# Expert stage: gate and up projections four blocks ahead in one PSUM bank, token rows turned six ahead, sixteen weight places

## The reference

```python
x = x + attn(xn, w_qkv, w_proj) + ffn(xn, router_w, shared..., experts...)

logits = hidden @ router_w                         # 64 experts
affinity = sigmoid(logits)
top_scores, top_idx = top_k(affinity, 8)           # 8 experts a token
top_w = top_scores / (sum(top_scores) + 1e-9)
gate_out = einsum('bsh,ehi->bsei', hidden, expert_gate_k)   # 256 -> 128
up_out = einsum('bsh,ehi->bsei', hidden, expert_up_k)       # 256 -> 128
expert_act = silu(gate_out) * up_out
routed = einsum('bsei,eih->bsh', expert_act * router_mask[..., None], expert_down_k)
shared = (silu(hidden @ sgw) * (hidden @ suw)) @ sdw
```

## Time and profile before

| | before |
|---|---|
| median of 3 runs | 1426.3 us (1416.28 to 1426.62) |
| the profiled execution | 1423.97 us |
| its span, first to last instruction | 1421.5 us |
| TensorE busy | 1156.4 us, 81% |
| DVE busy | 795.5 us, 56% |
| ACT busy | 756.0 us, 53% |
| GpSimd busy | 648.6 us, 46% |
| mean granted TensorE clock | 0.96 |
| bytes moved by DMA | 213.85 MB, 150 GB/s on average |

### The profile page before, as it was taken

One profiled execution on the slowest core, in us unless ns is written; L12 is line 12 of the kernel. 1 busy time (PEld: TensorE's weight loads), 2 busy tenths in 40 slices (PEclk: granted clock), 3 DMA queues, 4 the chain that ended last, 5 costly groups with the idle time before them and its releaser, 6 DMA issues. The chain is left out here.

```text
span 1421.5 us, 35722 instructions
## 1 busy us (share of the span) xinstructions
PE 1156.4 (81%) x8297; PEld 818.3 (58%) x8298; DVE 795.5 (56%) x2512; ACT 756.0 (53%) x1914; POOL 648.6 (46%) x658
## 2 busy tenths in 40 slices
PE   6987994878788878788888789778787788887889
PEld 3543563777777777677777778333344444444447
DVE  7877893333333333333333334777777777777733
ACT  3554673555555555555555557255454454545553
POOL 1443144444444444444444443555555555555520
PEclk9999997899999999999999999799999999999999
DMA  7887002666666666666666653254544455544413
GB/s 223 219 213 195 12 12 74 184 195 189 176 197 191 194 197 174 187 189 193 194 204 204 195 165 121 87 132 121 134 120 117 110 138 120 134 115 113 116 44 119
DMA packets 143770, 213.85 MB, mean 150 GB/s; under 512 B 20193, under 2 KB 116449, under 8 KB 143714
## 3 DMA queue, kind: packets, MB, share of 16 engines
q1 hardware_dynamic: 115234, 126.38, 30.7%
q0 software_dynamic: 27648, 86.02, 23.3%
q10 hardware_dynamic: 832, 0.79, 0.2%
HBM read 243.26 MB, written 70.26 MB: 221 GB/s over the span
## 5 line engine op out<-in xcount | busy, mean ns | idle before, releaser
L1038 POOL DMA_INDIRECT xb<-token_rows,idx_ring_x x320 | 303.2, 947 | 334.4 <-DVE ys L1166 223.5
L1656 POOL DMA_INDIRECT yg<-expert_rows,idx_ring x256 | 265.5, 1037 | 207.9 <-PE psum L1365 119.3
L1069 PE MATMUL psum<-xTe,wgu 128*128 128x128 f32 x2560 | 348.2, 280 | 7.6 <-issue 7.6
L1486 ACT ACTIVATE pT<-psum 128x384 f32<-128x384 f32 (+1 forms) x512 | 211.2, 467 | 243.0 <-PE psum L1365 228.1
L1069 PEld LDWEIGHTS psum<-xTe,wgu 128*128 128x128 f32 x2560 | 319.8, 196 | 11.6 <-issue 11.6
L1079 PE MATMUL psum<-wb,aT 128*128 x640 | 204.4, 402 | 114.8 <-DVE aT L1157 97.7
L1551 DVE CUSTOM_DVE_ANT_0 masked<-psum,mask_q 128x384 f32<-128x384 f32 (+1 forms) x512 | 247.6, 519 | 89.6 <-PE psum L1372 81.7
L1157 DVE TENSOR_TENSOR aT<-gate,psum 128x128 f32<-128x128 f32 x320 | 91.6, 286 | 312.2 <-remote 112.7
L1166 DVE TENSOR_SCALAR ys<-psum,xb 128x256 f32<-128x256 f32 x320 | 154.7, 484 | 111.7 <-PE psum L1079 91.3
L1380 PE MATMUL psum<-qk 98*128 98x384 bf16 (+1 forms) x512 | 169.4, 332 | 55.7 <-ACT pT L1486 50.0
L1372 PE MATMUL psum<-qk 96*128 96x384 bf16 (+1 forms) x512 | 172.3, 339 | 41.3 <-DVE xT_all_or_onorm L1580 12.4
(11 more groups left out here) (143 smaller groups left out, 1121.8 us busy)
## 6 DMA issues: line engine op xcount, KB each, us to landing
wb<-in_w_exp SPq DMA_DIRECT2D x320, 384.0 KB
expert_rows<-ys SPq DMA_DIRECT2D x160, 256.0 KB
qk<-q_stacks SPq DMA_DIRECT2D x32, 384.0 KB
q_stacks<-wb SPq DMA_DIRECT2D x32, 192.0 KB, 2.7
qk<-k_parts SPq DMA_DIRECT2D x32, 192.0 KB
k_parts<-wb SPq DMA_DIRECT2D x28, 192.0 KB, 3.1
token_rows<-rows SPq DMA_DIRECT2D x8, 640.0 KB, 4.6
xb<-token_rows,idx_ring_x POOLq DMA_INDIRECT x320
```

Of the source, the lines that this page charges most:

```text
L1038: nc.gpsimd.indirect_dma_start(out=xb[:, r, :], out_offset=None, in_=rows_d, in_offset=bass.IndirectOffsetOnAxis(ap=idx_ring[:, q, r:r + 1 ...
L1069: last = nc.tensor.matmul(banks[bank + r % 2][:, 0:P], wgu[:, r % NW, h, part * I:(part + 1) * I], xT[:, r % 2, h, :], start=(h == 0), sto ...
L1486: nc.scalar.activation(pT[:, (j % 2) * HG + hh, 0:(hi - lo) * P], key_bank(j, hh)[:, 0:(hi - lo) * P], ACT.Exp).then_inc(p_ready, 1)
L1656: nc.gpsimd.indirect_dma_start(out=yg[:, h, k, :], out_offset=None, in_=y_d, in_offset=bass.IndirectOffsetOnAxis(ap=idx_ring[:, h, k:k + 1 ...
```

## The change

Gate and up of a block go to the two halves of one PSUM bank and raise one semaphore, `gu_ready`, after the last of them. The four banks G and U become four banks GU, taken by r % 4; `xT`, `gate` and `aT` have four buffers instead of two. In step r TensorE does down(r), turn_x(r + 6), gate_up(r + 4); ACT does silu(r + 3), copy_x(r + 6), copy_w(r + 6); DVE does take_y(r), product(r + 3). PX and Y keep two banks. `wb` gets 16 places instead of 8. The eight more, and `wgu`, lie in the memory of `xT_all_or_onorm`, which the stages before and after use; so the first 8 places are loaded in `route` as before, and SyncE loads the other 8 at the head of `experts`. From then on weights are loaded 16 blocks ahead.

```diff
-WR = 8
+WR = 16
+WARM = 8
...
+            load = fields(sp, meta[:, LOAD_F, :], WR - WARM, WARM, (WR << PLACE_BIT) - 1)
+            for r in range(WARM, WR):
+                load_weights(sp, keep, w_exp, r, load[r - WARM])
             step(0)
...
             def turn_x(i, r):
                 pe.wait_ge(x_in[r % XR], i * 16 + 16 * (r // XR + 1))
-
-                if not first(i) or r > 1:
-                    pe.wait_ge(xT_ready, i * XR + (r - 1))
+                reach(pe, xT_ready, i, r - 1)
...
             def gate_up(i, r):
                 pe.wait_ge(wgu_ready, i * XR + r + 1)
                 pe.wait_ge(xT_ready, i * XR + r + 1)
-                if not first(i) or r > 1:
-                    pe.wait_ge(act_ready, i * XR + (r - 1))
-                for part, bank, ready in ((0, G, g_ready), (1, U, u_ready)):
+                reach(pe, act_ready, i, r - NB + 1)
+                for part in range(2):
                     for h in range(2):
-                        last = nc.tensor.matmul(banks[bank + r % 2][:, 0:P],
-                                                wgu[:, r % NW, h, part * I:(part + 1) * I], xT[:, r % 2, h, :],
+                        last = nc.tensor.matmul(banks[GU + r % NB][:, part * P:(part + 1) * P],
+                                                wgu[:, r % NW, h, part * I:(part + 1) * I], xT[:, r % NX, h, :],
                                                 start=(h == 0), stop=(h == 1))
-                    last.then_inc(ready, 1)
+                last.then_inc(gu_ready, 1)
...
                 for r in range(XR):
                     down(i, r, at[r])
-                    if exists(i, r + 3):
-                        turn_x(i, r + 3)
-                    if exists(i, r + 2):
-                        gate_up(i, r + 2)
-
-            for r in range(3):
+                    if exists(i, r + XLEAD):
+                        turn_x(i, r + XLEAD)
+                    if exists(i, r + LEAD):
+                        gate_up(i, r + LEAD)
+
+            for r in range(XLEAD):
                 turn_x(0, r)
-                if r > 0:
-                    gate_up(0, r - 1)
+                if r >= XLEAD - LEAD:
+                    gate_up(0, r - (XLEAD - LEAD))
...
                 for r in range(XR):
-                    if exists(i, r + 3):
-                        copy_x(i, r + 3)
-                    if exists(i, r + 2):
-                        silu(i, r + 2)
-                    if exists(i, r + NW):
-                        copy_w(i, r + NW, at[r + NW])
...
+                    if exists(i, r + LEAD - 1):
+                        silu(i, r + LEAD - 1)
+                    if exists(i, r + XLEAD):
+                        copy_x(i, r + XLEAD)
+                        copy_w(i, r + XLEAD, at[r + XLEAD])
...
                 for r in range(XR):
-                    if exists(i, r + 1):
-                        product(i, r + 1)
                     take_y(i, r, e[r])
-
-            product(0, 0)
+                    if exists(i, r + LEAD - 1):
+                        product(i, r + LEAD - 1)
+
+            for r in range(LEAD - 1):
+                product(0, r)
...
+        both = sb("wb_and_xT_all_or_onorm", [P, WARM * WCOLS + 2 * NTOK])
+        big = both[:, WARM * WCOLS:].rearrange("p (h n) -> p h n", h=2)
+        keep["wb"], keep["spare"] = both[:, 0:WR * WCOLS], both[:, WR * WCOLS:]
```

More of the change, by code:

```diff
@@ L662, in sync @@
         sp.wait_ge(meta_in, 16)
-        load = fields(sp, meta[:, LOAD_F, :], WR, 0, (WR << PLACE_BIT) - 1)
-        for r in range(WR):
+        load = fields(sp, meta[:, LOAD_F, :], WARM, 0, (WR << PLACE_BIT) - 1)
+        for r in range(WARM):
             load_weights(sp, keep, w_exp, r, load[r])
@@ L985, in exists, with reach @@
         return not isinstance(i, int) or i * XR + r < NB_ROUTED
+    def reach(engine, semaphore, i, n):
+        if not first(i) or n > 0:
+            engine.wait_ge(semaphore, i * XR + n)
     def every(engine, step):
@@ L1100, in copy_x @@
             def copy_x(i, r):
-                if not first(i) or r > 1:
-                    act.wait_ge(u_ready, i * XR + (r - 1))
+                reach(act, gu_ready, i, r - NX + 1)
                 act.wait_ge(px_ready, i * XR + r + 1)
-                nc.scalar.copy(xT[:, r % 2, :, :].rearrange("p h q -> p (h q)"), banks[PX + r % 2][:, 0:D]
+                nc.scalar.copy(xT[:, r % NX, :, :].rearrange("p h q -> p (h q)"), banks[PX + r % 2][:, 0:D]
                                ).then_inc(xT_ready, 1)
             def silu(i, r):
-                if not first(i) or r > 1:
-                    act.wait_ge(act_ready, i * XR + (r - 1))
-                act.wait_ge(g_ready, i * XR + r + 1)
-                nc.scalar.activation(gate[:, r % 2, :], banks[G + r % 2][:, 0:P], ACT.Silu).then_inc(gate_ready, 1)
+                reach(act, act_ready, i, r - NB + 1)
+                act.wait_ge(gu_ready, i * XR + r + 1)
+                nc.scalar.activation(gate[:, r % NB, :], banks[GU + r % NB][:, 0:P], ACT.Silu).then_inc(gate_ready, 1)
             def copy_w(i, r, at):
                 act.wait_ge(w_in[r % WR], i * (16 * XR // WR) + 16 * (r // WR + 1))
-                if not first(i) or r >= NW:
-                    act.wait_ge(u_ready, i * XR + (r - NW + 1))
+                reach(act, gu_ready, i, r - NW + 1)
                 nc.scalar.copy(wgu[:, r % NW, :, :].rearrange("p h c -> p (h c)"), wb[:, bass.ds(at, 4 * I)]
@@ L1152, in product @@
                 dve.wait_ge(gate_ready, i * XR + r + 1)
-                dve.wait_ge(u_ready, i * XR + r + 1)
-                if not first(i) or r > 1:
-                    dve.wait_ge(y_ready, i * XR + (r - 1))
-                nc.vector.tensor_tensor(aT[:, r % 2, :], gate[:, r % 2, :], banks[U + r % 2][:, 0:P], ALU.mult
+                reach(dve, y_ready, i, r - NB + 1)
+                nc.vector.tensor_tensor(aT[:, r % NB, :], gate[:, r % NB, :], banks[GU + r % NB][:, P:2 * P], ALU.mult
                                         ).then_inc(act_ready, 1)
```

52 lines of the change are left out of this document (24 added, 28 removed).

## The result

| | before | changed |
|---|---|---|
| median beside the first result (4 runs each) | 1423.5 us | 1385.4 us (1381.7 to 1391.7) |
| ratio | | 0.9739, 95% interval 0.9711 to 0.9767 |
| span of the profiled execution | 1421.5 us | 1379.7 us |
| first down projection starts at | 235.8 us | 240.8 us |
| last down projection starts at | 890.6 us | 849.2 us |

The change was forecast at 1350 us with a range of 1283 to 1430, faster with a chance of 0.74. It is faster, by about half of what was forecast. The whole gain lies in the experts' loop: 654.8 us between the first and the last down projection became 608.4, the first down projection starts 4.9 us later, and attention, which nothing in the change touches, stayed as it was.

The account below looks back on a forecast made before the run. TensorE's experts' loop was taken as bound by 148 us of waiting for results seen late because of closely spaced gathers. Saving 75 us and losing 2 at the head: 1424 - 73 = 1351, called 1350 us, range 1283 to 1430.

Parts of the forecast that it names:

- The stretch from 870 us on: Window 870 to 889 us of the earlier trace: no gather runs, TensorE has no gap, and no result comes late.
- Rival 2: Nothing moves: TensorE truly slower while transfers run, experts' loop stays at 2.04 us a block; 1424 to 1430 us; chance 0.14.
- no other engine is full: Experts' loop, per block: ACT has 1.27 us, GpSimd 0.95 us (1.24 at closest pace), DMA share 0.64.
- rival 1: All waiting in the experts' loop goes, 0 to 0.3 us left per cycle: 1278 to 1309 us, about 1290; chance 0.22.
- Gate and up four ahead: Experts' loop: product wanted two blocks, 3.09 us, later, so the down projection's wait for it goes.
- (a) to (c): Waits left in the loop: Y banks 0.29 us, PX banks none, ACT about 0.4 us; together 0.7 us per three blocks.
- Step (a): Y banks, still two: late take_y makes the down projection two blocks later wait 0.29 us.
- (c): ACT, in order, stands still 1.69 us and regains 1.3 us in three blocks; about 0.4 us stay.
- (1.44 - 0.7) x 101 = 75 us: Saving in the experts' loop: stall per three-block cycle falls from 1.44 to 0.7 us, over 101 cycles.
- rival 3: Slower loop: long rows of gathers 1.24 us apart, lateness beyond 2 us, SyncE also full; 1505 or 1460 us; chance 0.12.
- the likeliest case: Part of the loop's wait stays, 0.2 to 1.25 us per cycle: 1300 to 1405 us, point 1350; chance 0.52.
- The merging: Gate and up in one bank, three announcements a block instead of four: between nothing and a quarter of lateness, counted as nothing.

Follow-up runs that it names:

- experiment 6: Changed kernel with GpSimd's row gathers left out after the first 16 blocks, held condition: 1276.5 us; kernel before beside it 1401.7 us.
- experiments 4 and 11: 4: changed kernel plus one GpSimd memset behind each gather, 1170.1 us. 11: changed kernel without weight loads after the first 16 places, 1170.5 us.
- experiment 12: Changed kernel with results of two neighbouring down projections in the halves of one Y bank, free condition: 1169.8 us against 1174.4 us, ratio 0.9962.
- experiment 10: Kernel before with only gate and up merged into one bank with one announcement, free condition: 1179.9 us against 1172.3 us, ratio 1.007.
- experiment 8: Changed kernel with two GpSimd memsets behind each gather, each waited for, free condition: 1359.9 us against 1172.3 us, ratio 1.160.

## Why the prediction was right or wrong

**What bounds the kernel.** Right in the held condition, in which all that I had was taken: 148 us of waiting in the loop, results seen late by ACT and DVE, tied to the gathers (experiment 6: without them all 1.546 us). Wrong was to take this for a property of how closely the gathers follow one another. In the free condition twelve gathers in a row come under 1.35 us apart (experiments 4 and 11) and hold nothing; in the changed kernel in the held one, behind the first twenty, there are never more than five. The stretch from 870 us on in the earlier trace rows, which I read as the proof, goes with gathers being needed for it (experiment 6 shows that), not with their being enough. Rival 2, a truly slower TensorE, is out: the same matmuls run at 1.546 us wherever no gather holds them.

Wrong was also "no other engine is full", which left SyncE out. Of the 148 us "that an edit of waits can win", SyncE had only 75 us of waiting for results in blocks 10 to 300; with its own 1.79 us a block it stood close behind. So rival 1, which wanted 115 to 146 us, was out of reach unless SyncE's instructions became less stretched.

**Gate and up four ahead.** Right: TensorE's wait for aT fell from 96.1 to 17.1 us, and the products would have held up none of the 91 long steps that are left, where they ended 95 of 105 before. This was the step that carried the sign.

**What is late next, (a) to (c).** Right in the place, wrong in the size, and this is the term of the sum that was off. Step (a) named the Y banks, and all stalls that could be put down end with take_y. But it kept the lateness of before, 1.9 us, and came to 0.29 us a stall, with 0.4 us for (c), 0.7 us for three blocks. Measured are 104.1 us for 289 blocks, 1.08 us for three. The term (1.44 - 0.7) x 101 = 75 us measured 143.9 - 104.1 = 40 us. The stalls did not shrink to 0.7 us each either: there are 91 of 1.14 us on average, against 105 of 1.37. The lateness did not keep still: take_y starts 1.53 us behind its down projection instead of 0.37 (medians), and up to 4.5 us. Two things lie in it: TensorE announces later (a median of 0.73 us behind the end of the matmul instead of 0.33), while gathers come in tighter groups (under 1.4 us from the last in 53% of the cases instead of 24%), and stores land late, for which take_y waits 99.1 us. How the single stalls divide between the two is not known. But what the loop takes in all is set by SyncE, which has no waiting left in it: had TensorE announced sooner and SyncE's instructions been as stretched as they are, take_y would have waited longer for its stores. This follows from the trace; no run tried it. That the forecast is within 3% of the measured time is therefore partly luck: its sum holds no term for SyncE, and 75 us happens to be what SyncE had to give before its own time grew.

**SyncE.** The text had this under rival 3 only, as part of a kernel that gets slower. It is what bounds the likeliest case. Register instructions of SyncE that take more than 0.15 us, and gaps of more than 0.15 us ahead of them and of DMA issues, without a wait of their own, add up to 213 us in blocks 10 to 300 before, to 259 us changed, and to 4 us without gathers (experiment 6) or in the free condition (experiment 12). With this SyncE's own time rose from 1.79 to 1.91 us a block, 35 us in these blocks, and the gain in them is 41 us and not 75. That the rest of rival 3 did not come, with the gathers feeding on one another until the loop passes 2.036 us, fits with the take_y that is late, since it holds back the gathers too; no run tests it.

**The merging.** I counted nothing. It costs 0.7% without the longer lead in the free condition (experiment 10), and there the lead covers it.

**Sixteen places.** Right that they win nothing (0.0 us of idle ahead of the weight copies), that the eight loads take SyncE 4 to 9 us (6.2 us) and that the head loses: 4.9 us at the first down projection, of which 0.8 us are left by the eleventh, against 2 with a range of 0 to 9.

**The rest.** Attention unchanged within 0.4 us, as assumed. The rule on regular bubbles (the Trainium skill, Trainium Kernel Development and Optimization, Best Practices) did not decide: more buffers took the bubble from aT and left it at the Y banks, with SyncE full behind them. In the free condition the kernel before, with the same two buffers, takes only about 4 us more than experiments 4 and 12. The rule that SyncE's transfers stay clear of the path of GpSimd's descriptors (the Trainium skill, DMA: Bandwidth & Descriptors, SWDGE vs HWDGE vs iDMA) goes with the free condition, 0.86 us for two loads; in the held one SyncE does stand still beside gathers, 1.19 to 2.27 us for two, and no run here shows by what way.

## What to carry to other kernels

Where consumers start long after the matmul that they wait for was over, count how late they are and see which ring between the engines is too short for it: lengthening one moves the stall to the next, here from aT to the Y banks at about 70% of its size (104.1 of 143.9 us). Before that, take each engine's own time per block, the one that only issues transfers too, and the waiting that it has left: here SyncE's 75 us were the most that any longer ring could win, and the change used them up. And time the kernel before next to each variant: the same kernel was 250 us apart between two sets, six times what the change is worth.

## What the runs showed of the hardware

- The same kernel takes 1402 to 1433 us or 1171 to 1176 us, in sets of runs minutes apart, and within a set always the same. One chip showed both. What sets it is open; every variant was run beside the kernel before, and none changed the condition. The time ahead of the first gather does not differ: TensorE is busy for 189.9 us of the first 226 in both (the changed kernel, and experiment 8).
- In the held condition GpSimd's gathers go with late announcements of TensorE (more than 40 ns behind the matmul in 535 of 997 cases in the loop before, 572 of 790 in that of the changed kernel, 480 of 727 in the attention of experiment 6; the median of the changed kernel is 0.73 us, the longest 2.8 us) and stretch many of SyncE's register instructions to about 0.7 us each. ACT and DVE are spared: 3 and 4 us in the loop before against SyncE's 213, by the same count, and none of their announcements in the changed kernel's loop is late (0 of 618 and 0 of 453). It ends where the gathers end, within one execution.
- In the free condition attention is not quite free of it: 122 of 982 announcements (experiment 12, 750 to 1100 us) come more than 40 ns late, the longest 0.7 us.
- The matmul rows of the profile give no hint of it: they stay 0.11 us apart and their ends, which are modelled, are on time; only what is released by them is late. Whether the results themselves or only the news of them come late is open. Attention is hit too: 530.9 us from the last down projection to the end, against 436.6 us in the free condition.
- In the held condition the trace also lacks records of semaphore updates wherever gathers run: 256 of take_y's 320 are there in the changed kernel, and all of them in experiment 12. In experiment 6 the loop without gathers lacks 1 of 2381 (260 to 720 us), attention with its gathers 524 of 1901 (760 to 1100 us). So the two may have one cause, and since every run on record has a span and a clock from the profiler, it is not tested whether the recording itself has a part in the held condition.
